# First stage of a graph-attention kernel: two small tables turned into rows through HBM instead of through TensorE

## The reference, cut to what matters

```python
def gnn(x, src, dst, W, a_src, a_dst):              # N=6250 nodes, E=100000 edges sorted by dst
    h = einsum('ni,hio->hno', x, W)                 # 8 heads, 256 -> 32
    s, d = einsum('hno,ho->hn', h, a_src), einsum('hno,ho->hn', h, a_dst)
    w = exp(leaky_relu(s[:, src] + d[:, dst]) - max)
    out = segment_sum(w / (segment_sum(w)[dst] + 1e-10) * h[:, src], dst)
    return out + x
x = x + gnn(layernorm(x), src, dst, ...)
x = x + moe_ffn(layernorm(x), ...)                  # 16 experts, top 2, then a layernorm
```

## Time and profile before

| | |
|---|---|
| time, median of 3 runs | 1986.72 us (1985.87 to 1988.36) |
| profiled execution: time / span | 1983.17 us / 1981.4 us |
| TensorE granted clock, mean of the span | 0.734 of full speed |
| first stage | about 0 to 97 us |
| edge loop | about 97 to 1350 us |

### The profile page before, as it was taken

One profiled execution on the slowest core, in us unless ns is written; L12 is line 12 of the kernel. 1 busy time (PEld: TensorE's weight loads), 2 busy tenths in 40 slices (PEclk: granted clock), 3 DMA queues, 4 the chain that ended last, 5 costly groups with the idle time before them and its releaser, 6 DMA issues.

```text
span 1981.4 us, 28027 instructions
## 1 busy us (share of the span) xinstructions
PE 1518.3 (77%) x6733; PEld 1113.7 (56%) x6733; DVE 1177.7 (59%) x3449; ACT 775.5 (39%) x2346; POOL 1213.1 (61%) x1197
## 2 busy tenths in 40 slices
PE   3927777777777777777777777673968999999975
PEld 2714444444444444444444444442848999999963
DVE  5746666666666666666666666668983444333338
ACT  2624444444444444444444444432622233223326
POOL 4066666666666666666666666645364776666757
PEclk9956666666666666766656666766559999999987
DMA  6544444444444444444444444432856878877876
GB/s 184 164 120 115 120 112 113 115 117 118 112 115 114 117 118 110 114 115 117 118 111 115 114 119 114 115 79 80 252 168 184 226 212 210 213 210 203 217 170 200
DMA packets 166686, 284.19 MB, mean 143 GB/s; under 512 B 31760, under 2 KB 93285, under 8 KB 166373
## 3 DMA queue, kind: packets, MB, share of 16 engines
q0 software_dynamic: 62256, 143.99, 30.5%
q1 hardware_dynamic: 101908, 137.90, 21.9%
q10 hardware_dynamic: 2368, 0.52, 0.2%
HBM read 240.97 MB, written 42.16 MB: 143 GB/s over the span
## 4 chain that ended last, share of the span: by engine, by line
PE 63%; DVE 18%; issue 8%; DVEq 3%; another core or an unknown queue 3%; POOL 2%; DMA 1%; ACT 1%; ACTq 0%; POOLq 0%; SPq 0%
PE bank L1057 29%; PE bank L1198 10%; PE bank L1210 10%; DVE region L1518 4%; PE bank L1046 3%; PE bank L1082 3%; PE bank L990 2%; DVE z L1471 2%; DVE region L1516 2%; DVEq L494 2%; PE bank L1043 2%; POOL region L925 1%; DVE z L1478 1%; DVE z L1483 1%
## 5 line engine op out<-in xcount | busy, mean ns | idle before, releaser
L895 POOL DMA_INDIRECT region<-node_rows,region x832 | 790.5, 950 | 483.7 <-issue 222.7
L1057 PE MATMUL bank<-region 128*128 128x264 f32 x1664 | 746.7, 597 | 84.5 <-DVE region L1518 81.3
L1057 PEld LDWEIGHTS bank<-region 128*128 128x128 f32 x1664 | 440.5, 290 | 224.2 <-issue 138.4
L1518 DVE TENSOR_TENSOR region<-region,bank 128x264 f32 x728 | 311.5, 428 | 354.3 <-PE bank L1057 269.0
L748 ACT ACTIVATE neg_max<-bank 128x1 f32<-128x1 f32 x104 | 17.8, 171 | 723.1 <-PE bank L1082 593.6
L1504 DVE TENSOR_TENSOR region<-region,bank 128x512 f32<-128x512 f32 x416 | 265.9, 681 | 7.2 <-ACT bank L755 4.8
L738 ACT ACTIVATE region<-iota_row,region 128x128 f32<-128x128 f32 x832 | 262.7, 386 | 0.0
L822 ACT ACTIVATE region<-bank,b_col 128x128 f32<-128x128 f32 x452 | 129.0, 368 | 311.6 <-PE bank L1198 210.6
L971 POOL DMA_INDIRECT sum_rows<-region,row_u x113 | 180.0, 1593 | 111.5 <-DVE region L1938 45.2
L1198 PEld LDWEIGHTS bank<-region 128*128 128x128 f32 x1808 | 220.1, 192 | 6.3 <-issue 0.4
L1198 PE MATMUL bank<-region 128*128 128x128 f32 x1808 | 220.7, 275 | 0.2 <-issue 0.2
(11 more groups left out here) (246 smaller groups left out, 1618.4 us busy)
## 6 DMA issues: line engine op xcount, KB each, us to landing
region<-in_L_ffn_w SPq DMA_DIRECT2D x129, 512.0 KB, 8.4
region<-dloc_rows SPq DMA_DIRECT2D x104, 256.0 KB
region<-node_rows,region POOLq DMA_INDIRECT x832
node_rows<-region SPq DMA_DIRECT2D x12, 528.0 KB
y_rows<-region SPq DMA_DIRECT2D x7, 896.0 KB, 5.5
sum_rows<-region SPq DMA_DIRECT2D x7, 896.0 KB, 7.7
region<-in_x SPq DMA_DIRECT2D x5, 896.0 KB, 12.4
region<-sum_rows SPq DMA_DIRECT2D x5, 896.0 KB, 11.1
```

The source lines that it names most:

```text
L895: p.indirect_dma_start(gathered[g % SLOTS][:, j, :], None, node_rows, bass.IndirectOffsetOnAxis(src_idx[:, k:k + 1], 0)).then_inc(row_in[g ...
L1057: pe.matmul(bank[AGG_BANKS[k % AGG]][:, 0:ROW], onehot[:, (g % 3) * GROUP + j, :], gathered[g % SLOTS][:, j, :], start=True, stop=True).th ...
L1518: v.tensor_tensor(rows, rows, new, ALU.add).then_inc(acc_add)
```

## The change

The 14 transposes, their semaphore and VectorE's four copies out of PSUM go away. VectorE makes an int32 copy of `step_tc` (128 by 7, `step_tci`) at t = 12. SP stores `step_tci` and `step_t` to two HBM tables of 896 elements at t = 17, element by element (each run is 4 bytes, since a column of the table is a row in HBM), and at t = 33 waits for both stores and loads `tile_row` (896 contiguous elements) and `tfirst` (104 single elements, every eighth). Whoever waited for the rows now waits for these loads, or for `step_tci` where the wait only kept an order.

```diff
--- before.py
+++ after.py
@@ -73,6 +73,8 @@
         node_rows = dram("node_rows", [TILES * P, ROW])
         y0_rows = dram("y0_rows", [TILES * P, Y_ROW])
         sum_rows = dram("sum_rows", [(TILES + 3) * P, F_IN])
+        step_tiles = dram("step_tiles", [STEP_BLOCKS * P], I32)
+        step_firsts = dram("step_firsts", [STEP_BLOCKS * P])
         src_pad = dram("src_pad", [CHUNKS * P], I32)
         dst_pad = dram("dst_pad", [CHUNKS * P], I32)
         dloc_rows = dram("dloc_rows", [STEP_BLOCKS * P, P], BF16)
@@ -176,6 +178,7 @@
         step_t = sb("step_t", [P, STEP_BLOCKS])
         step_t128 = sb("step_t128", [P, STEP_BLOCKS])
         step_tc = sb("step_tc", [P, STEP_BLOCKS])
+        step_tci = sb("step_tci", [P, STEP_BLOCKS], I32)
         tile_row = sb("tile_row", [1, STEP_BLOCKS * P], I32)
         tfirst = sb("tfirst", [1, GROUPS])
         attn_dst = sb("attn_dst", [P, TILES, HEADS])
@@ -274,7 +277,7 @@
         x_tail_zero = sem("x_tail_zero")
 
         ends_step, chunk_out, chunk_in = sem("ends_step"), sem("chunk_out"), sem("chunk_in")
-        table_step, tile_tr = sem("table_step"), sem("tile_tr")
+        table_step, tables_out, tile_row_in, tfirst_in = sem("table_step"), sem("tables_out"), sem("tile_row_in"), sem("tfirst_in")
         rows_f32, rows_tr, rows_sb = sem("rows_f32"), sem("rows_tr"), sem("rows_sb")
         w_by_a_ok, w_cat_step = sem("w_by_a_ok"), sem("w_cat_step")
 
@@ -332,7 +335,7 @@
         CONSTS = at(["iota_f", "consts", "far_zero", "inits"])
         TABLE = at([("count", b) for b in range(STEP_BLOCKS)] + [("step_c", b) for b in range(STEP_BLOCKS)]
                    + ["step_ci"] + [("delta", b) for b in range(STEP_BLOCKS)]
-                   + ["step_t", "step_tc", "tile_row", "tfirst"])
+                   + ["step_t", "step_tc", "step_tci"])
         PART = at(["hi", "rest0", "mid", "rest1", "lo"])
         LATE = at(["late", "late_plus", "late_min", "late_top", "eps_row", "eps", "base0"])
         SUMS = at([(name, n) for n in range(len(C_PARTS)) for name in ("sums", "rsum")])
@@ -390,6 +393,7 @@
 
         COUNT_AT, DELTA_AT, FIRST_AT = 8, 10, 12
         ROWS_AT = [20 + 3 * b for b in range(STEP_BLOCKS)]
+        STEP_TABLES_OUT_AT, STEP_TABLES_IN_AT = 17, 33
         H_GROUP = 4
         H_OUTS = (TILES - 1) // H_GROUP + 1
 
@@ -570,6 +574,15 @@
                         d.dma_start(b1_rows[:, :], b1).then_inc(b1_in, 16)
                         d.dma_start(gamma_bc[:, :], gamma.partition_broadcast(P)).then_inc(b1_in, 16)
                         d.dma_start(beta_bc[:, :], beta.partition_broadcast(P)).then_inc(b1_in, 16)
+                if t == STEP_TABLES_OUT_AT:
+                    d.wait_ge(table_step, TABLE["step_tci"])
+                    d.dma_start(step_tiles.rearrange("(b p) -> p b", p=P), step_tci[:, :]).then_inc(tables_out, 16)
+                    d.dma_start(step_firsts.rearrange("(b p) -> p b", p=P), step_t[:, :]).then_inc(tables_out, 16)
+                if t == STEP_TABLES_IN_AT:
+                    d.wait_ge(tables_out, 32)
+                    d.dma_start(tile_row[0:1, :], step_tiles.rearrange("(a k) -> a k", a=1)).then_inc(tile_row_in, 16)
+                    d.dma_start(tfirst[0:1, :].unsqueeze(2), step_firsts[0:STEPS].rearrange(
+                        "(a g j) -> a g j", a=1, j=GROUP)[:, :, 0:1]).then_inc(tfirst_in, 16)
                 if t in ROWS_AT:
                     n = ROWS_AT.index(t)
                     d.wait_ge(rows_b_ok, n + 1)
@@ -995,12 +1008,6 @@
             pe.matmul(bank[4][0:CHUNK_PARTS, 0:1], before[0:CHUNK_PARTS, 0:CHUNK_PARTS],
                       counts[:, 1, CHUNK_COLS - 1:CHUNK_COLS], start=True, stop=True).then_inc(ends_step)
             for t in range(TILES):
-                if t == FIRST_AT:
-                    pe.wait_ge(table_step, TABLE["step_tc"])
-                    for n, col in enumerate((step_tc, step_t)):
-                        for b in range(STEP_BLOCKS):
-                            pe.transpose(bank[4 + 2 * n + b // 4][0:1, (b % 4) * P:(b % 4 + 1) * P],
-                                         col[:, b:b + 1], ident[:, :]).then_inc(tile_tr)
                 if t in ROWS_AT:
                     b = ROWS_AT.index(t)
                     for n in range(2):
@@ -1009,7 +1016,7 @@
                         if b >= 2:
                             pe.wait_ge(rows_sb, 2 * (b - 2) + n + 1)
                         elif b == 0:
-                            pe.wait_ge(table_step, TABLE["tfirst"])
+                            pe.wait_ge(table_step, TABLE["step_tci"])
                         pe.transpose(bank[4 + slot][:, 0:P], rows_f[:, slot, :], ident[:, :]).then_inc(rows_tr)
                 pe.wait_ge(xn_ok, t + 1)
                 if t >= 2:
@@ -1059,9 +1066,9 @@
             pe.wait_ge(xnt_ok, TILES)
 
             pe.wait_ge(rows_sb, 2 * STEP_BLOCKS)
-            pe.wait_ge(table_step, TABLE["tfirst"])
+            pe.wait_ge(tfirst_in, 16)
             pe.matmul(bank[M_BANK][:, 256:256 + GROUPS], ones[0:1, :], tfirst[:, :], start=True, stop=True).then_inc(late_mm)
-            pe.wait_ge(table_step, TABLE["tile_row"])
+            pe.wait_ge(tile_row_in, 16)
             attn_dst_of(0, tiles_of(pe, mybir.EngineType.PE, 0 * GROUP, GROUP))
             for g in range(GROUPS + 1):
                 now, more = g < GROUPS, g + 1 < GROUPS
@@ -1339,16 +1346,8 @@
                     v.wait_ge(table_step, TABLE["step_t"])
                     v.tensor_scalar(step_t128[:, :], step_t[:, :], float(P), None, ALU.mult)
                     v.tensor_scalar(step_tc[:, :], step_t[:, :], float(TILES - 1), None, ALU.min).then_inc(table_step)
-                elif t == FIRST_AT + 3:
-                    half = 512 // GROUP
-                    v.wait_ge(tile_tr, STEP_BLOCKS)
-                    v.tensor_copy(tile_row[:, 0:512], bank[4][0:1, :])
-                    v.tensor_copy(tile_row[:, 512:STEP_BLOCKS * P],
-                                  bank[5][0:1, 0:STEP_BLOCKS * P - 512]).then_inc(table_step)
-                    v.wait_ge(tile_tr, 2 * STEP_BLOCKS)
-                    v.tensor_copy(tfirst[:, 0:half], bank[6][0:1, 0:512:GROUP])
-                    v.tensor_copy(tfirst[:, half:GROUPS],
-                                  bank[7][0:1, 0:(GROUPS - half) * GROUP:GROUP]).then_inc(table_step)
+                    v.wait_ge(table_step, TABLE["step_tc"])
+                    v.tensor_copy(step_tci[:, :], step_tc[:, :]).then_inc(table_step)
                 elif t in ROWS_AT:
                     b = ROWS_AT.index(t)
                     v.wait_ge(rows_in[b], 32)
@@ -1404,7 +1403,7 @@
                                    ALU.mult).then_inc(scale_ok)
 
 
-            v.wait_ge(table_step, TABLE["tfirst"])
+            v.wait_ge(table_step, TABLE["step_tci"])
             for t in range(0, TILES, BATCH):
                 v.memset(acc[:, t * ROW:(t + BATCH) * ROW], 0.0).then_inc(acc_zero)
 
@@ -1551,7 +1550,7 @@
                     if n % GROUP == 0:
                         if k == 0:
                             v.wait_ge(acc_zero, 7)
-                            v.wait_ge(table_step, TABLE["tile_row"])
+                            v.wait_ge(tile_row_in, 16)
                         tiles = tiles_of(v, mybir.EngineType.DVE, k, min(GROUP, len(steps) - n))
                     yield add_step(k, tiles[n % GROUP])
             for g in range(GROUPS + 1):
```

## The result

The changed kernel is slower: 1992.11 us median (1989.1 to 1995.11, 10 runs) against 1985.86 us (1983.57 to 1988.36, 10 runs) of the kernel before beside it on the same chip. The ratio is 1.0035 with a 95% interval of 1.0026 to 1.0043, some 6 us lost where 12.8 were forecast as a gain. The time lies above the range of 1966 to 1985. The profiled execution took 1991.82 us with a span of 1990.0.

The account below looks back on a forecast made before the run. The prediction took TensorE's pace to bound the first stage, with a hole ahead from late delivery of 14 transposes. It summed -13.8 + 1.0 = -12.8 us, from 1986.7 to 1973.9 us, range 1966 to 1985.

Parts of the forecast that it names:

- the whole -13.8 us: First stage, tiles 12 to 14: removing the 14 transposes brings tile 14's transform from 54.97 to 41.14, 13.8 us earlier.
- rival 1: First stage: the hole is not the transposes', perhaps POOL's 14 gathers'; only 0 to 2 us come; chance 0.10.
- The equal halves: Hole behind the transposes: two readers 6.28 and 6.35 us apart, read as 0.90 us for each of 14 transposes.
- kept the pace of 1.13 us: First stage from 30.01 on: transforms stayed 1.13 us apart while gathers already ran, an argument against the gathers as cause.
- The rule that I set against the rows: TensorE semaphores: 26.3 ns per increment, so the 14 transposes cost 2.0 us and the change gives 1984.7.
- I take **1.0: DMA queues behind the element stores: the store of tiles 16 to 19 late by 0 to 1.8 us, taken as 1.0.
- 0.020 us per run: Element stores at t = 17: run price from stores of 8-byte runs, giving 2.3 us of queue, landing in 3.6 us.
- priced at 42 us: Element stores' landing: the skill's 19 times for a rearranged DMA, taken on 2.2 us, would give 1992 us.
- rival 3: SP's wait at t = 33: element stores land so slowly that the gain is gone beyond 37 us; chance 0.03.
- The issue on SP: SP at t = 17: two store issues of 0.37 us each, 0.7 us hidden in 2.7 us of idle time.
- rival 4: Start of the edge loop: its waits of 13.05 and 7.28 us change; below 1966 chance 0.09, slower 0.04.
- rivals 1 and 2: The second: late stores hold ScalarE's copies more than once, giving 4 to 9 us back, 1977 to 1983; chance 0.10.

Follow-up runs that it names:

- stores alone: Kernel before, transposes kept, with the two element stores added at t = 17 and unused: 1981.79 us (1.0045) on one chip, 1990.38 us (1.0041) on another.
- fourth group: Four kernels on one chip with the hole, kernel before 1981.78 us: element stores unused, the same 64 bytes apart, the changed kernel, kernel before with 7 gathers.
- first group: Kernels taking the change's parts separately (rows left out, gathers delayed, only element stores, short-run stores with element loads), on one chip; kernel before 1972.76 us.
- the spread stores: Kernel before plus the two unused element stores, each element 64 bytes from the next: 1985.81 us, ratio 1.0016.
- the held kernel: Changed kernel without its stores and loads (rows zeroed), POOL's gathers of blocks 3 to 6 waiting for tile 16 normalised: 1971.80 us, ratio 0.9997 to before.
- the chain above: Chain that ended last in the kernel before with 7 gathers replacing 14, transposes kept: 1973.80 us, ratio 0.9956; the transposes take 1.83 us of it.
- other kernels with element stores: Kernels beside the changed one's first measurement that write single 4-byte elements, such as the kernel before with unused element stores: 1981.79 us, ratio 1.0045.
- the six comparisons: The result's own measurement and five sets of follow-up kernels, each beside the kernel before: 1985.86, 1972.76, 1973.40, 1778.09, 1981.78 and 1777.95 us.
- third group: Four kernels on a chip without the hole, kernel before 1778.09 us: element stores 64 bytes apart (1.0016) and three kernels with 7 gathers (0.9999 to 1.0007).
- fifth group: Two kernels with 7 gathers, kernel before 1777.95 us: with transposes 1777.82 us (1.0004), with short-run stores and element loads 1779.58 us (1.0007).

## Why the prediction was wrong

**The step that failed:** "So I take the delivery of these 14 results as the cause", the whole -13.8 us. The wait was real, and so was its place on the chain. But its owner was POOL's run of 14 gathers, named as rival 1 and given 0.10. Two arguments against that rival misled me.

*The equal halves.* 6.28 and 6.35 us in the earlier trace rows looked like 0.90 us for each transpose. The distances don't follow the transposes. In the kernel with the stores alone of the fourth group, the same two readers come like this:

```profile
49.10 0.68 DVE L1352 CAST tile_row<-bank 1x512 int32<-1x512 f32 x1 [11.77 <-remote]
...
50.66 0.21 DVE L1356 COPY tfirst<-bank 1x64 f32<-1x64 f32 x1 [0.41 <-remote]
```

Waits of 11.77 and 0.41 us, for the same 14 transposes: the first reader starts 9.80 us after them, the second 1.56 us after that. In the first group's stores alone it is 3.89 and 5.64 us, with the spread stores of the fourth 5.25 and 5.72. The halves were one observation of one execution.

*"TensorE and ScalarE kept the pace of 1.13 us from 30.01 on with these gathers already running".* That was true of the first six gathers at most, and not even there throughout: the trace has TensorE idle for 2.98 us up to 35.21, between its transforms of 31.14 and 35.48. In these traces the results become late after about that many have been issued back to back, and the held kernel, which pauses behind the sixth, has its late results in the second run. The gathers' end (46.76 + 0.95 = 47.71) and the hole's end (50.2) lie 2.5 us apart in the kernel before; with the run shifted to end at 50.59, the hole ended at 52.3.

The rule that I set against the rows, the Trainium skill's 26.3 ns for each increment ("TensorE: Matmul & The Clock Gate", section "The cost: per-tile semaphore tail"), fits where I had said that the trace disagreed by a factor of thirty. With it the estimate was 2.0 us for the 14 transposes in all, 1.5 of them from rows; the chain above has 1.83.

**The mis-sized term:** "I take **1.0**" for the stores, with bounds 0 and 1.8. By themselves they cost 8.6 us in the fourth group and 9.0 in the first (1981.79 - 1972.76). The step under it was 0.020 us per run, read off stores of 8-byte runs; I carried it to runs of half the size and to another layout, as if a run were a run. The landing was forecast at 3.6 us and was 10.2 and 12.2 in the kernel with the stores alone of the fourth group, 11.2 and 13.5 in that of the first. The mechanism in the forecast was right in each link: SP's order, the store of tiles 16 to 19 behind them, ScalarE's copy of tile 24. Only the price was not. The rule of the Trainium skill that I priced at 42 us ("DMA: Bandwidth & Descriptors", section "Rules for kernel authors") pointed to the right side and was too high by a factor of three to four. That the case built on it in rival 3 came to 1992 us, the measured time, is luck: its place of loss, SP's wait at t = 33, was not seen, and the hole that it took to be gone was still there.

**The issue on SP** was taken at 0.37 us each, hidden in a gap of 2.7. It took 0.63 and 2.64, and then 5.08 for the store behind and 2.60 for the load behind that. In the other kernels with element stores the store behind took 2.30 to 2.83 us. SP itself became busy, which no row of before showed.

**The other steps** held. VectorE's copies were worth nothing. The loads at t = 33 went unseen: their issue starts right behind that of the `dloc_rows` store before them, with no gap of SP (rival 3's place). The edge loop began as before (rival 4): from the last weight load of the transforms to the first of the aggregation it is 38.8 us, and 37.5 before.

**The chances.** I gave rivals 1 and 2 0.10 each as if they excluded one another. What happened is both: no gain from the hole, and 8 to 9 us from a store that holds ScalarE. That sum, 1986.7 + 8.6 - 1.8 = 1993.5, is near the 1992.1 that was measured, and it stood nowhere among the cases. Slower had 0.07, all of it from other mechanisms.

The sum with measured terms: -0.6 to -1.8 for the transposes, +8.6 for the stores, together 6.8 to 8.0 us. Measured: 6.3 for the result, 5.7 in the fourth group. That is 0.5 to 2.3 us less, within the width of these intervals.

**What stays open.** By which way POOL's gathers delay TensorE's results, why they do so in four of the six comparisons (in one of them read from the gain alone) and not in the two on quicker chips (in one of them read from the missing gain alone), and from which number of gathers on. What neighbouring 4-byte writes do to one another in HBM was seen by its price only. Whether the rows through short runs beat the transposes once the hole is gone was compared side by side only on two chips of the kind without it; on chips with it each was run in a different group (0.9956 with the transposes, 0.9951 without).

## What to carry to other kernels

When several engines wait at one time and the releaser is unknown, ask which engine was busy in all of it, even if it shares no semaphore with the waiters, and take it away in an experiment before the work that stands next to the hole is rewritten. Where a DMA has to transpose a small table, try the single elements on the reading side first: here short contiguous writes and single-element reads cost nothing that could be told. And when two rivals act on different terms of the sum, their joint case belongs among the cases.

## What the hardware showed that I had not expected

- 1,792 writes of 4 bytes into neighbouring addresses landed in 10.2 and 12.2 us; 64 bytes apart they landed in 5.2 and 7.4. Written as 256 runs of 28 bytes, with 1,000 reads of 4 bytes on the way back, the tables cost nothing measurable. The DMA behind the 4-byte writes took 2.30 to 5.08 us to issue in four traces instead of 0.37, and 2.50 behind the spread ones: that part does not need neighbouring addresses.
- With a run of 14 indirect DMAs issued back to back by POOL, TensorE's results reached ScalarE and VectorE late, after waits of 2 to 12 us. With 7 of twice the row size they did not, nor with 14 in pairs spaced apart (0.9956 and 0.9951, 0.9954).
- This is a property of the chip too. In the third group's trace with 14 gathers there is no such hole, and the whole kernel took 1778 us there and in the fifth group, where the others took 1973 to 1986.
